# Making the values on POOL, and moving the search's products and readings, in a sparse attention kernel with a feed-forward part

## What is computed

```python
scores = jnp.einsum('bhqd,bhkd->bhqk', q, k) * scale
sparsity = scores.max(axis=-1) - scores.mean(axis=-1)
_, top_idx = jax.lax.top_k(sparsity, U)          # U = 307 of 4096
...
attn = jax.nn.softmax(scores_sel, axis=-1)
out_sel = jnp.einsum('bhuk,bhkd->bhud', attn, v)
...
x = layernorm(x + attn_out); x = layernorm(x + r * (relu(k)**2 @ W_v.T))
```

## Time and profile before

| | |
|---|---|
| Time, median of 3 runs | 3397.01 us (3394.32 to 3403.04) |
| The profiled execution's own time | 3401.7 us |
| Its span, first to last instruction | 3400.0 us |
| Busy: PE, DVE, ACT, POOL | 90%, 87%, 83%, 44% |
| Mean granted clock of TensorE | 0.962 |
| First and last maximum start | 63.5 and 3087.1 us |

### The profile page before, as it was taken

The page is one execution under the profiler, slowest core; times in us unless marked ns, Lnnn a source line. Parts: engine busy times, 40 slices in busy tenths (PEclk is TensorE's granted clock), DMA queues, the critical chain, the costliest instruction groups (busy, mean ns, idle before and its releaser), DMA issues.

```text
span 3400.0 us, 60106 instructions
## 1 busy us (share of the span) xinstructions
PE 3059.6 (90%) x16612; PEld 1461.9 (43%) x16612; DVE 2965.4 (87%) x6028; ACT 2813.0 (83%) x6118; POOL 1504.7 (44%) x2616
## 2 busy tenths in 40 slices
PE   6999899877999999999999899899998899997587
PEld 3333333333444444444434455544444444444366
DVE  4999999867899899899989899889998899896588
ACT  5999889866898899799899788699987699894455
POOL 3210022100453464464345474576554564556654
PEclk8999999989899999899999999999999999997799
DMA  6343233321242114123121224222141023112022
GB/s 181 82 120 106 59 79 88 77 7 20 45 34 28 26 33 39 30 36 33 26 39 33 54 53 29 45 44 39 36 44 38 20 39 33 33 21 13 15 81 70
DMA packets 263681, 163.71 MB, mean 48 GB/s; under 512 B 168946, under 2 KB 242866, under 8 KB 259250
## 3 DMA queue, kind: packets, MB, share of 16 engines
q1 hardware_dynamic: 255250, 156.41, 24.9%
q0 software_dynamic: 6144, 1.37, 0.5%
q10 hardware_dynamic: 1952, 2.10, 0.2%
HBM read 111.86 MB, written 47.86 MB: 47 GB/s over the span
## 4 chain that ended last, share of the span: by engine, by line
DVE 37%; PE 27%; ACT 18%; issue 15%; POOL 2%; DMA 1%; ACTq 0%; DVEq 0%; SPq 0%; POOLq 0%
DVE JK L1163 29%; ACT AB L1009 15%; PE DP L743 7%; PE CP L739 4%; PE CP L730 4%; DVE SPr L1163 1%; ACT E L1044 1%; PE BP L761 1%; PE PV L851 1%; DVE VF L1375 1%; PE PV L852 1%; PE BP L815 1%; PE BP L836 1%; PE PV L874 1%; DVE fst L1334 1%
## 5 line engine op out<-in xcount | busy, mean ns | idle before, releaser
L1163 DVE CUSTOM_DVE_ANT_0 JK<-DP,AB 128x1024 bf16<-128x1024 f32 x2048 | 2464.5, 1222 | 207.5 <-ACT AB L1009 76.9
L1009 ACT ACTIVATE AB<-CP 128x512 f32<-128x512 f32 x4096 | 2296.9, 624 | 312.5 <-PE CP L730 215.4
L743 PE MATMUL DP<-KS,QS 128*128 128x512 f16 x4096 | 1246.3, 386 | 61.0 <-DVE SPr L1163 54.9
L1588 POOL TENSOR_TENSOR SCR<-E 128x307 f16<-128x307 f32 x966 | 672.3, 708 | 536.3 <-ACT E L1044 529.1
L739 PE MATMUL CP<-KS,QS 128*128 128x512 f16 x2048 | 800.6, 391 | 31.8 <-ACT AB L1009 0.4
L730 PE MATMUL CP<-KS,QS 128*128 128x512 f16 x2048 | 799.5, 390 | 30.9 <-DMA QS<-QSC 14.1
L743 PEld LDWEIGHTS DP<-KS,QS 128*128 128x128 f16 x4096 | 362.8, 98 | 396.1 <-DVE SPr L1163 177.9
L1044 ACT ACTIVATE E<-BP 128x307 f32<-128x307 f32 x916 | 438.6, 479 | 44.6 <-PE BP L836 40.3
L730 PEld LDWEIGHTS CP<-KS,QS 128*128 128x128 f16 x2048 | 203.3, 99 | 440.5 <-ACT AB L1009 354.4
L739 PEld LDWEIGHTS CP<-KS,QS 128*128 128x128 f16 x2048 | 198.8, 97 | 375.9 <-ACT AB L1009 324.2
L836 PE MATMUL BP<-QT,KA 128*128 128x307 f16 x916 | 271.3, 296 | 20.3 <-ACT QT L1036 19.2
(11 more groups left out here) (383 smaller groups left out, 3190.0 us busy)
## 6 DMA issues: line engine op xcount, KB each, us to landing
KS<-KTC SPq DMA_DIRECT2D x256, 128.0 KB
QS<-QSC SPq DMA_DIRECT2D x512, 64.0 KB
KA<-KTC SPq DMA_DIRECT2D x128, 128.0 KB
QN<-SCR SPq DMA_DIRECT2D x16, 544.0 KB, 3.4
SCR<-in_L_attn_x SPq DMA_DIRECT2D x16, 512.0 KB, 5.9
AO<-E SPq DMA_DIRECT2D x16, 512.0 KB, 7.2
VF<-in_L_attn_x SPq DMA_DIRECT2D x64, 128.0 KB, 2.2
VF<-AO SPq DMA_DIRECT2D x64, 128.0 KB, 2.2
```

Source lines behind the costliest of these rows:

```text
L743: r = pe.matmul(o[:, 512 * j:512 * j + 512], qs, ks[j][:, 0, :], start=True, stop=True)
L1009: act.activation(AB[p % 3][:, 512 * j:512 * j + 512], BANK["C%d" % j], ACT.Abs).then_inc(ab_full, 1)
L1163: dve.tensor_tensor_reduce(out=JK[p % 2][:], in0=BANK["D%d" % u], in1=AB[p % 3][:], scale=1.0, scalar=0.0, op0=ALU.add, op1=ALU.max, accum ...
L1588: pool.tensor_tensor(EL[a % NE], E[a % NE][:], EH[a % NE], ALU.subtract).then_inc(el_g, 1)
```

## The change

- **Values.** ACT writes the scaled product as f32 into one of four staging buffers, which lie in a scratch tile of the keys. POOL makes the f16 high half from it and then the low half. DVE no longer takes part, the product's bank is free after ACT, and attention, a later input load on SP and the clearing of scratch on POOL wait for POOL's semaphore `val_pool`.
- **Banks in turn.** Background products take `next_bank()`, which passes over the bank of the product before when there is more than one spare. Search products still take `bank()`.
- **The count.** Of a digit's three steps the gap now comes between comparison and count. A new token `second` does C0 and C1 of a step; count and digit follow, then `main` with D alone. The step still takes no other entry under the same condition.
- **Behind maxima.** `cut`, `need`, `rank1`, `rank2` and `idx` are one token each for PE and DVE, behind the step's `main`: DVE reads after the step's maximum.
- **Hold.** A step with one of these, or a flip, now holds two steps back, itself and the next.

```diff
+    def next_bank():
+        b = bank()
+        while len(spare) > 1 and b == state["before"]:
+            b = bank()
+        state["before"] = b
+        return b
...
         for i in range(len(DIGITS)):
             yield [("cmp", g, i, on)] + ([("sel", g, i)] if i < n else [])
+            for _ in range(gaps):
+                yield []
             bk = bank()
             yield [("cnt", g, i, bk), ("digit", g, i, on, bk)]
-            for _ in range(gaps):
-                yield []
...
-        yield both("cut")
+        yield [("cut", g, bank())]
...
             step = next(sel, None) or []
-            plan.extend(token for token in step if token[0] in EARLY)
+            if step and step[0][0] == "cnt":
+                plan.append(("second", n * NP + p))
+                plan.extend(step)
+                step = []
+                hold = 1 if "P" not in spare or "feed" in done else hold
             plan.append(("main", n * NP + p))
...
-            plan.extend(token for token in step if token[0] not in EARLY)
+            plan.extend(step)
             if ("P" not in spare or "feed" in done) and any(token[0] in ONE_BANK for token in step):
-                hold = 1
+                hold = 2
...
-                    owed[bank] = ((val_act, 32 * b + t + 1), (val_dve, 32 * b + t + 1))
+                    owed[bank] = ((val_act, 32 * b + t + 1),)
...
-            def main(p):
-                u = p % 2
+            def second(p):
                 if p not in led:
                     lead_(p)
+                seconded.add(p)
                 qs, ks = scores(p)
                 o = claim("C1")
                 pe.matmul(o, qs, ks[1][:, 1, :], start=True, stop=True).then_inc(sc_c, 1)
                 owed["C1"] = ((ab_full, 2 * p + 2),)
+
+            def main(p):
+                u = p % 2
+                if p not in seconded:
+                    second(p)
+                qs, ks = scores(p)
                 o = claim("D%d" % u)
...
             def vev(b, t, bank):
                 if t == 0:
-                    act.wait_ge(consts, 3)
+                    act.wait_ge(s_lo, 24 * (b + 1))
+                after(act, val_pool, NT * b + t - 3)
                 act.wait_ge(val_pe, NT * b + t + 1)
-                act.mul(V[b][1][:, t, :, 0:DH], BANK[bank][:, 0:D].rearrange("p (h d) -> p h d", d=DH),
-                        1.0 / WS).then_inc(val_act, 1)
+                act.mul(vstage[t % 4], BANK[bank][:, 0:D], 1.0 / WS).then_inc(val_act, 1)
...
-                dve.scalar_tensor_tensor(out=V[b][1][:, t, :, DH:2 * DH], in0=sv, scalar=1.0 / WS, in1=V[b][1][:, t, :, 0:DH],
-                                         op0=ALU.mult, op1=ALU.subtract).then_inc(val_dve, 1)
...
+            def vev(b, t, bank):
+                v = vstage[t % 4].rearrange("p (h d) -> p h d", d=DH)
+                hi, lo = (V[b][1][:, t, :, a:a + DH] for a in (0, DH))
+                pool.wait_ge(val_act, NT * b + t + 1)
+                pool.wait_ge(q_pool, seq.mark(dup(hi, v)))
+                pool.tensor_tensor(lo, v, hi, ALU.subtract).then_inc(val_pool, 1)
...
                 if b and c < 4:
                     sp.wait_ge(xt_pe, 16 * b)
                     sp.wait_ge(s_lo, 24 * b)
+                    sp.wait_ge(val_pool, NT * b)
```

More of the change, by code:

```diff
@@ L35 @@
 XW = 4 * 128 + 16
-ONE_BANK = ("flip", "cnt", "cut", "need", "rank1", "rank2", "idx")
-EARLY = ("digit", "cutv", "needv", "rank1v", "rank2v", "idxv")
+ONE_BANK = ("flip", "cut", "need", "rank1", "rank2", "idx")
 def after(engine, semaphore, value):
@@ L62, in schedule @@
     spare = ["B", "P", "D00", "D01", "D10", "D11", "C0", "C1"]
-    state = {"turn": 0, "open": None, "late": None, "search": False, "arranged": 0}
+    state = {"turn": 0, "open": None, "late": None, "search": False, "arranged": 0, "before": None}
     tail = [False]
@@ L82, in tokens @@
             for k in range(2):
-                bk = bank()
+                bk = next_bank()
                 evict = [("xtev", b, c, k, bk)]
@@ L196, in select @@
             yield [("cmp", g, i, on)] + ([("sel", g, i)] if i < n else [])
+            for _ in range(gaps):
+                yield []
             bk = bank()
             yield [("cnt", g, i, bk), ("digit", g, i, on, bk)]
-            for _ in range(gaps):
-                yield []
-        def both(stage, *args):
-            bk = bank()
-            return [(stage, g, *args, bk), (stage + "v", g, *args, bk)]
         for _ in range(2 * gaps):
             yield []
-        yield both("cut")
+        yield [("cut", g, bank())]
         for _ in range(3 * gaps):
             yield []
-        yield both("need")
-        yield both("rank1")
+        yield [("need", g, bank())]
+        yield [("rank1", g, bank())]
         for _ in range(4 * gaps):
             yield []
-        yield both("rank2")
+        yield [("rank2", g, bank())]
         yield [("slots", g)]
@@ L226, in select @@
         for h in range(n):
-            yield both("idx", h) + ([("ixdma", g, h, h + 1)] if tail[0] else [])
+            yield [("idx", g, h, bank())] + ([("ixdma", g, h, h + 1)] if tail[0] else [])
         if gaps:
@@ L300, in feed @@
                         if 0 <= k - n < NT:
-                            step.append((f, b, k - n, bank(), late))
+                            step.append((f, b, k - n, next_bank(), late))
                     if step:
@@ L923, in f7 @@
                     owed[bank] = ((f_o1, k + 1),)
-            stages = dict(xt=xt, kbar=kbar, ffw=ffw, kmm=kmm, qmm=qmm, qtr=qtr, val=val, lead=lead_, main=main, flip=flip, cnt=cnt, cut=cut, need=need_, rank1=rank1,
+            stages = dict(xt=xt, kbar=kbar, ffw=ffw, kmm=kmm, qmm=qmm, qtr=qtr, val=val, lead=lead_, second=second, main=main, flip=flip, cnt=cnt, cut=cut, need=need_, rank1=rank1,
                           rank2=rank2, idx=idx, qt=qt, st=st, pv=pv, otr=otr, f1=f1, f2=f2, f4=f4, f6=f6, f6k=f6k, f7=f7)
@@ L1242, in digit, with cut @@
                                   best[0:rows, 1:2].bitcast(I32), ALU.bitwise_or).then_inc(sel_thr, 1)
-            def cutv(g, bank):
+            def cut(g, bank):
                 n, _, (m1, m2, *_) = views(g)
@@ L1257, in needv, with rank1 @@
                 dve.tensor_scalar(need[:, 0:n], BANK[bank][:, 0:n], -1.0, float(U), ALU.mult, ALU.add).then_inc(sel_m, 1)
-            def rank1v(g, bank):
+            def rank1(g, bank):
                 n, _, (m1, m2, m3, *_) = views(g)
@@ L1268, in rank1v, with rank2 @@
                 dve.tensor_tensor(m3, m3, m1, ALU.add).then_inc(sel_m, 1)
-            def rank2v(g, bank):
+            def rank2(g, bank):
                 n, (_, _, m3f, sf, *_), _ = views(g)
@@ L1299, in oa, with idx @@
                     dve.tensor_scalar(OA[:, j, 0:NT * n], fa[:, 0:NT * n], float(j), None, ALU.is_equal).then_inc(sel_oa, 1)
-            def idxv(g, h, bank):
+            def idx(g, h, bank):
                 after(dve, l_i, 64 * g)
@@ L1405, in f9 @@
                                       ALU.mult).then_inc(f_o3, 1)
-            stages = dict(xtev=xtev, kbar=kbar, kev=kev, split=split, vev=vev, main=main, cap=capture, parts=parts, cmp=cmp,
-                          digit=digit, cutv=cutv, needv=needv, rank1v=rank1v, rank2v=rank2v, slots=slots, ob=ob, oa=oa, idxv=idxv,
+            stages = dict(xtev=xtev, kbar=kbar, kev=kev, split=split, main=main, cap=capture, parts=parts, cmp=cmp,
+                          digit=digit, cut=cut, need=need_, rank1=rank1, rank2=rank2, slots=slots, ob=ob, oa=oa, idx=idx,
                           st=st, otr=otr, f2=f2, f2s=f2s, f3=f3, f5=f5, f7=f7, f8=f8, f9=f9)
```

27 lines of the change are left out of this document (13 added, 14 removed).

## The result

| | before | after |
|---|---|---|
| Median | 3396.48 us (3394.32 to 3403.04, 4 runs) | 3361.05 us (3355.80 to 3361.51, 4 runs) |
| The profiled execution's own time | 3401.7 | 3360.67 |
| Its span | 3400.0 | 3358.7 |
| Mean granted clock | 0.962 | 0.972 |
| First and last maximum start | 63.5, 3087.1 | 61.5, 3036.9 |

The ratio is 0.9889 (95% interval 0.9872 to 0.9906). The forecast was 3371 in 3328 to 3405, faster. It holds in sign and in range, 10 us too high.

The account below looks back on a forecast made before the run. It found no engine full on average, DVE alone setting heads 2 and 3, and bank waits slowing head 7. Its terms (-44.5, -10.6, +24.6, +3.5, -9, +8) summed to -28.0, giving 3369; it took 3371, range 3328 to 3405.

Parts of the forecast that it names:

- Head 7: Head 7 loses its PE waits: digits 6.71 to 4.9 us, -27; behind them -12; with head 8, -44.5 in all.
- the low halves on DVE: Taking the values' low halves off DVE: counted as 21 us; in head 7 PE waited 17.1 us for them.
- Heads 2 and 3: Heads 2 and 3, where DVE is full: 32 low halves of 0.33 us leave it, -10.6 us.
- The digits under attention: Groups 1, 2, 3 and 6: the count's move makes a digit 4.98 us against 4.57, +24.6 in all.
- The first rival: Digits under attention and feed: delaying C0 costs nothing, intervals 4.5 us or less, total 3330; chance 0.25.
- the slower one: Every counted step: the ring of C0, count and D costs more, over 5.3 us a digit under attention; chance 0.13.
- The feed's digits: Groups 4 and 5, beside feed-forward work: net +3.5 us, bounds -20 and +20.
- the 0.25 a digit for the count's move: Groups 4 and 5: the count's move costs +0.25 us a digit, +7.5 in all.
- The turns of banks: Groups 4 and 5: taking banks in turn saves some 4 us, as 38 repeated claims of about 0.1.
- Readings and holds: Six groups: search products behind maxima, with the held steps' relief, save 1.5 us each, -9; bounds 0 and -24.
- The end: Behind the last maximum: steps pushed there by the hold of two cost +8 us, bounds 0 and +16.
- POOL in DVE's way: POOL's work lengthens DVE's small sum in head 7: +5 us, or up to +10, total 3378; chance 0.08.

Follow-up runs that it names:

- e2: The kernel before with one part alone, values made on POOL: 3343.85 us, ratio 0.9845.
- e3: The kernel before with both moves of the count alone (a step later, and between C1 and D): 3409.55 us, ratio 1.0049.
- e4: The changed kernel with the count back in its old place, keeping the readings behind maxima and the hold of two steps: 3338.62 us, ratio 0.9838.
- e12: e8 plus both moves of the count, with readings ahead of maxima and a hold of one step: 3358.06 us, ratio 0.9902.
- e8: The kernel before with values on POOL and banks in turn, nothing else of the change: 3313.44 us, ratio 0.9789.
- e1: The kernel before with one part alone, background products taking their banks in turn: 3348.12 us, ratio 0.9864.
- e7: e4 with a hold of one step in place of two, so e8 plus readings behind maxima: 3318.75 us, ratio 0.9805.

## Why the prediction was right, and where it was off

The forecast was right in its mechanism where most of the time went, in head 7 and in the digits under attention, and two of its smaller terms were not. The measured 41 us against 28 come for the most part from heads 7 and 8 and from the feed's digits.

**Head 7** was read rightly: banks by turns made P's eviction the one just queued. Its price came to -51.3 with head 8 against -44.5, since digits (4.74), the stretch ahead of them and head 8 came out a little better. Wrong was a step beside it, that the low halves on DVE were worth 21 us and the wait for them 17.1. e2 shows that the wait and the low clock went together, and that either part of the change cures most of the head.

**Heads 2 and 3** gave 6.7 in place of 10.6. I had taken DVE as the only full engine there and ACT's copy as costing nothing. DVE's timeline in head 2, which answers to the earlier trace rows:

```profile
280.87 1.22 DVE L1170 CUSTOM_DVE_ANT_0 JK<-DP,AB 128x1024 bf16<-128x1024 f32 x1
...
282.01 1.22 DVE L1170 CUSTOM_DVE_ANT_0 JK<-DP,AB 128x1024 bf16<-128x1024 f32 x1
...
283.25 1.23 DVE L1170 CUSTOM_DVE_ANT_0 JK<-DP,AB 128x1024 bf16<-128x1024 f32 x1
```

and ACT's:

```profile
280.78 1.09 ACT L1022 ACTIVATE AB<-CP 128x512 f32<-128x512 f32 x2
281.76 0.38 ACT L1016 ACTIVATE SCR<-BP 128x256 f32<-128x256 f32 x1
282.03 3.37 ACT L1022 ACTIVATE AB<-CP 128x512 f32<-128x512 f32 x6
285.30 0.38 ACT L1016 ACTIVATE SCR<-PV 128x256 f32<-128x256 f32 x1
```

Copy to copy is 3.54 us for three steps, where DVE could do them in 3 x 1.15 = 3.45. ACT idles only twice in it, 0.05 us each, for C0. With the low halves gone ACT and C0 are the next limit: from one absolute of C0 to the next it is 1.14 us, and 1.25 where a copy lies between. So each copy costs about 0.1 of the 0.33 that its low half gave back. Head 2 gave 4.9 of its 22 x 0.33 = 7.3, and head 3, with 10 low halves, 1.8 of 3.3.

**The digits under attention** are the best confirmed term: 5.01 in place of 4.98, with ACT idle 0.63 where 0.7 was named, +22.8 in place of +24.6. The first rival (the delay costs nothing) wanted 4.5 or less and the slower one over 5.3; neither came. e3, e4 and e12 show that the cost is the count's. Some of the agreement is luck. The working was done for a group of five heads and used for all four groups. In groups of three the counting products take 0.54 to 0.57 us, not 0.78, and groups 2 and 6 ran at clock 0.95 in after; in e12, at 1.00, 1.00 and 0.98, the same moves cost 0.31, 0.16 and 0.36 in groups 2, 3 and 6.

**The feed's digits** were +3.5 and are -3.0, well inside their bounds of 20. The step that failed is the 0.25 a digit for the count's move, +7.5: between e4 and after it costs 0.01 and 0.03 a digit, between e8 and e12 0.10 and 0.06, and in e3 0.04 and -0.08, so -0.6 to +2.4 us in all. The turns of banks, -4 in the prediction, are -5.9 in e1.

**Readings and holds** had the right sum by luck. Of the -9.1 measured, -5.8 lie in the feed's four heads, and there e1, with banks in turn alone, already has -7.2 outside digits. The readings behind maxima (e7 against e8) show no gain, and head 14 has a loss that no term held.

**The end** at +8.9 is near the +8 worked out for the hold, but not all of it is the hold's: 6.7 are (e4 less e7), and 3.7 come with the count's moves (after less e4).

**POOL in DVE's way** did not come where I looked for it. The small sum ahead of a digit, in head 7 and then in group 1, answers to the earlier trace rows:

```profile
L1225 DVE TENSOR_SCALAR ahead_of<-steps,test 120x2 f32<-120x2 f32 x12 | 2.7, 225 | 0.0
...
L1225 DVE TENSOR_SCALAR ahead_of<-steps,test 120x2 f32<-120x2 f32 x12 | 2.7, 226 | 0.0
```

It is short in both: the count's new place puts the sum behind POOL's low half of an exponential (which starts at 963.38, 0.70 long; the sum starts at 964.20), where the old one had it beside, at 551 ns. With POOL making the values and the count in its old place (e8) the sum takes 415 ns in head 7 and 483 in group 1, and in e12 225 and 228: so the price that I looked for is real, and the count's move hides it. The loss came in head 14 instead.

## What to carry to other kernels

A change of several parts is to be priced part by part, and its parts run alone: here two of them give 0.9789, the others take half of that back (0.9889), and the total alone would have praised them all. Before moving a small product, ask what its queue has behind it: a count that must wait for a bank holds up every product behind it, and doubling it shows in one run whether it has cover, though not which of several waits it lengthens. Work that is held back beside a full loop is not free: here it was paid behind the loop. And where a wait goes together with a lower clock, as in head 7, the products that run slower belong in its price.

## What the runs showed of the hardware that was not expected

- A pair of DVE tensor_scalars of 128x96 f16, 0.27 us otherwise, took 4.79 us in e4 beside back-to-back tensor_tensors on POOL; seven of POOL's instructions passed before the second one ended. In e7 two of the same kind took 0.56 and 0.74 us, so it is not always so. A sum of 120x2 took 0.55 us or 0.23 according to whether POOL worked at that moment.
- ACT's 128x512 absolute values last 0.6 us each, but start 0.48 to 0.49 after each other where the second one's product is there. Where ACT had to wait even 0.05 us for it, the distance was 0.65: six take 3.37 us with two such waits. A copy of 128x256, 0.38 long, adds 0.26 to the row.
- With a wait of 17.1 us for DVE gone (e2), the granted clock of that head was 1.00 in place of 0.87, and PE's busy time was 17 us less, about as much again as the wait.
